# Self attention in a 6-stage decoder kernel: one PSUM bank for both halves of the transposed probabilities, three banks in rotation instead of two

## The reference, cut to what matters

```python
Q = (x @ Wq.T + bq).reshape(B, N, H, HD)
K = (x @ Wk.T + bk).reshape(B, N, H, HD)
V = (x @ Wv.T + bv).reshape(B, N, H, HD)
scores = jnp.einsum('bnhd,bmhd->bhnm', Q, K)
scores = scores * (SCALE * adaptive_scale)[None, :, None, None] / TEMP
w = jax.nn.softmax(scores, axis=-1)
attn = jnp.einsum('bhnm,bmhd->bnhd', w, V).reshape(B, N, H * HD)
y = x + (attn @ Wo.T + bo)
return (y - mu) / jnp.sqrt(var + EPS) * gamma + beta
```

## Time and profile before

| What | Value |
|---|---|
| Median of 3 runs | 1846.4 us (1839.13 to 1853.87) |
| The profiled execution, its own time | 1854.84 us |
| Its span, first to last instruction | 1853.1 us |
| Mean granted TensorE clock | 0.933 |
| Self attention, first scores to the last layer norm | about 1114 to 1605 us |
| DMA over the whole span | 8 to 9 GB/s |

### The profile page before, as it was taken

One profiled execution on the slowest core, in us unless ns is written; L12 is line 12 of the kernel. 1 busy time (PEld: TensorE's weight loads), 2 busy tenths in 40 slices (PEclk: granted clock), 3 DMA queues, 4 the chain that ended last, 5 costly groups with the idle time before them and its releaser, 6 DMA issues. The chain is left out here.

```text
span 1853.1 us, 28867 instructions
## 1 busy us (share of the span) xinstructions
PE 1646.3 (89%) x10524; PEld 949.1 (51%) x10524; DVE 1260.1 (68%) x1701; ACT 1202.8 (65%) x2569; POOL 481.8 (26%) x402
## 2 busy tenths in 40 slices
PE   5999999999999964888879798999999999789985
PEld 2343444444444422666656535666666566466654
DVE  2778777777777767888815555666666666588854
ACT  3787887787787743788772365555655556377754
POOL 2111011111111134777620002222222222155530
PEclk9999999999999975899995689999999999799977
DMA  3000001000000021000000000000000000000001
GB/s 131 1 12 1 0 7 24 0 0 0 1 0 1 0 48 30 5 6 9 2 2 1 0 1 1 1 1 1 1 1 1 1 1 1 8 8 8 2 1 46
DMA packets 30529, 16.99 MB, mean 9 GB/s; under 512 B 8545, under 2 KB 29246, under 8 KB 30398
## 3 DMA queue, kind: packets, MB, share of 16 engines
q1 hardware_dynamic: 27710, 10.52, 2.3%
q10 hardware_dynamic: 2688, 4.72, 0.7%
HBM read 13.14 MB, written 2.10 MB: 8 GB/s over the span
## 5 line engine op out<-in xcount | busy, mean ns | idle before, releaser
L2247 POOL TENSOR_TENSOR self_probs<-self_probs,self_rz 128x1024 f32<-128x1024 f32 x64 | 121.3, 1895 | 488.9 <-DVE self_rz L2278 488.9
L558 POOL TENSOR_SCALAR gru_decay<-gru_zgate 128x512 f32<-128x512 f32 x96 | 75.2, 783 | 563.1 <-ACT gru_zgate L509 537.1
L2222 ACT ACTIVATE self_probs<-self_scores,self_neg 128x128 f32<-128x128 f32 x512 | 181.4, 383 | 16.8 <-DVE self_neg L2273 16.8
L417 PE MATMUL gru_gate<-gru_xn,gru_whg 128*128 128x512 f32 x384 | 182.2, 597 | 3.5 <-DVE gru_xn L605 3.5
L421 PE MATMUL gru_hid<-gru_xn,gru_whg 128*128 128x512 f32 x384 | 180.4, 592 | 0.0
L429 PE MATMUL gru_out<-gru_y,gru_wo 128*128 128x512 f32 x384 | 178.1, 599 | 0.7 <-DVE gru_y L635 0.6
L1385 ACT ACTIVATE x_pt<-x_turned 77x512 f32<-77x512 f32 x256 | 137.6, 585 | 60.3 <-PE x_turned L1282 59.0
L1282 PE MATMUL x_turned<-const_ident,x_probs 128*77 128x128 f32 x1024 | 147.5, 290 | 20.8 <-POOL x_probs L1434 11.5
L1282 PEld LDWEIGHTS x_turned<-const_ident,x_probs 128*77 128x77 f32 x1024 | 119.6, 154 | 73.2 <-POOL x_probs L1434 25.9
L630 DVE SCALAR_TENSOR_TENSOR gru_ghid<-gru_hid,gru_half_c,gru_sighid 128x512 f32<-128x512 f32 x96 | 71.7, 747 | 107.9 <-ACT gru_sighid L510 107.8
L1491 DVE TENSOR_REDUCE x_m<-x_scores 128x16 f32<-128x1232 f32 x64 | 91.7, 1432 | 49.9 <-PE x_scores L1271 48.6
(11 more groups left out here) (440 smaller groups left out, 3507.7 us busy)
## 6 DMA issues: line engine op xcount, KB each, us to landing
gru_whg<-in_L_attn_Whg ACTq DMA_DIRECT2D x4, 768.0 KB, 9.5
x0e_ctx_in<-in_ctx SPq DMA_DIRECT2D x16, 154.0 KB
gru_xin<-in_x SPq DMA_DIRECT2D x8, 256.0 KB, 2.9
out<-moe_y SPq DMA_DIRECT2D x8, 256.0 KB, 2.2
gru_wo<-in_L_attn_Wo ACTq DMA_DIRECT2D x4, 384.0 KB, 10.6
selfe_raw<-in_L_attn_Wq SPq DMA_DIRECT2D x1, 512.0 KB, 4.5
selfe_raw<-in_L_attn_Wk SPq DMA_DIRECT2D x1, 512.0 KB, 5.7
selfe_raw<-in_L_attn_Wv SPq DMA_DIRECT2D x1, 512.0 KB, 6.8
```

Source lines behind the costliest of these rows:

```text
L417: mm(ps_gate[n % 2][:, :], whg[:, l, k, DI + c * P:DI + (c + 1) * P], xn[u][:, k, :], start=(k == 0), stop=(k == KH - 1))
L2222: last = f(probs[n % 2][:, a, jj, :], ps_s[n % 2][:, a, jj * T:(jj + 1) * T], ACT.Exp, bias=neg[n % 2][:, a, jj:jj + 1], accum_out=z[n % 2 ...
L2247: pool.tensor_tensor(probs[n % 2][:, :, :, :], probs[n % 2][:, :, :, :], whole, ALU.mult).then_inc(pn_ready.sem, 1)
```

## The change

The two banks `turned0` and `turned1` become one, `turned`; the bank set free joins the rotation, which now has three (`NBANKS`). Since both halves go through one bank, PE waits before half 1 for DVE's copy of half 0 of the same step, and before half 0 for the copy of half 1 of the step before. In `ORDER`, half 1 of `turn` moves behind `norm` x+1 and `scores` x+2. No operation is added or taken away.

```diff
-        ps_t = [t.ps(f"turned{e}", [P, 512]) for e in range(2)]
-        bank = [t.ps(f"bank{r}", [P, 512]) for r in range(2)]
+        ps_t = t.ps("turned", [P, 512])
+        NBANKS = 3
+        bank = [t.ps(f"bank{r}", [P, 512]) for r in range(NBANKS)]
...
             if now:
-                ORDER += [("turn", x, 0, 0), ("turn", x, 1, 0)]
+                ORDER += [("turn", x, 0, 0)]
             if x + 1 < LAST:
                 ORDER += [("norm", x + 1, 0, 0)]
             if later:
                 ORDER += [("scores", x + 2, 0, 0)]
+            if now:
+                ORDER += [("turn", x, 1, 0)]
...
             source = (op[0][:-4],) + op[1:]
-            r = TURN[source] % 2
-            engine.wait_ge(filled[r].sem, TURN[source] // 2 + 1)
+            r = TURN[source] % NBANKS
+            engine.wait_ge(filled[r].sem, TURN[source] // NBANKS + 1)
             return bank[r], freed[r].sem
...
                         pe.wait_ge(pn_ready.sem, n + 1)
-                        if n:
-                            pe.wait_ge(pt_ready[a].sem, n)
+
+                        if a:
+                            pe.wait_ge(pt_ready[0].sem, n + 1)
+                        elif n:
+                            pe.wait_ge(pt_ready[1].sem, n)
                         for jj in range(HALF):
-                            last = turn(ps_t[a][:, jj * T:(jj + 1) * T], probs[n % 2][:, a, jj, :], ident[:, :])
+                            last = turn(ps_t[:, jj * T:(jj + 1) * T], probs[n % 2][:, a, jj, :], ident[:, :])
```

More of the change, by code:

```diff
@@ L2010, in self_attention_stage @@
         pn_ready = t.count("pn_ready")
-        filled = [t.count(f"filled{r}") for r in range(2)]
-        freed = [t.count(f"freed{r}") for r in range(2)]
+        filled = [t.count(f"filled{r}") for r in range(NBANKS)]
+        freed = [t.count(f"freed{r}") for r in range(NBANKS)]
         sq_ready = t.count("sq_ready")
@@ L2097, in shared @@
             source = (op[0][:-4],) + op[1:]
-            r = TURN[source] % 2
-            engine.wait_ge(filled[r].sem, TURN[source] // 2 + 1)
+            r = TURN[source] % NBANKS
+            engine.wait_ge(filled[r].sem, TURN[source] // NBANKS + 1)
             return bank[r], freed[r].sem
         def taken(engine, *ops):
-            for r in range(2):
-                counts = [TURN[op] // 2 + 1 for op in ops if TURN[op] % 2 == r]
+            for r in range(NBANKS):
+                counts = [TURN[op] // NBANKS + 1 for op in ops if TURN[op] % NBANKS == r]
                 if counts:
@@ L2126, in _ @@
                     if op in TURN:
-                        r, before = TURN[op] % 2, TURN[op] // 2
+                        r, before = TURN[op] % NBANKS, TURN[op] // NBANKS
                         to = bank[r]
@@ L2280, in _ @@
                         if n >= 2 and a == 0:
-                            r, at = TURN["attend", n - 2, 0, 0] % 2, TURN["attend", n - 2, 0, 0] // 2
+                            r, at = TURN["attend", n - 2, 0, 0] % NBANKS, TURN["attend", n - 2, 0, 0] // NBANKS
                             dve.wait_ge(filled[r].sem, at + 1)
                         dve.wait_ge(turned[a].sem, n + 1)
-                        v.tensor_copy(pt[n % 2][:, a, :, :].rearrange("p j t -> p (j t)"), ps_t[a][:, :]).then_inc(pt_ready[a].sem, 1)
+                        v.tensor_copy(pt[n % 2][:, a, :, :].rearrange("p j t -> p (j t)"), ps_t[:, :]).then_inc(pt_ready[a].sem, 1)
                     elif kind == "attend_out":
```

## The result

The changed kernel took 1833.5 us (median, 1819.6 to 1841.0) beside 1849.4 us for the kernel before in the same series; the ratio is 0.9908, with a 95% interval of 0.9888 to 0.9929. That is 17 us, 0.92%, where the forecast had 19 us, 1.02%. The interval leaves out a ratio of 1, so the kernel is faster; but the gain is just short of the 1% from which the forecast would call it so. The profiled execution took 1837.25 us, against 1854.84 us.

A forecast was written before the change was run, and what follows sets the result against it. PE was taken to set the pace, losing 3.3 us per eight steps to full banks. Terms -16.5 - 6.3 + 3.0 = -19.8, taken as -19 off the 1846.4 median: 1827.4 us, range 1814 to 1848.

The forecast's parts named there:

- The middle: Six full groups of eight steps in self attention: 57.5 in place of 60.28 us each, -16.5 us in all.
- 3.3 us in eight steps are lost to full banks: PE's eight steps take 60.28 us against 57.0 unhindered; three banks were to take the full 3.3 us off.
- The new wait: Half 1 of `turn` waits for half 0's copy; the scores cover it with 0.2 us to spare, nothing charged.
- R1: Rival: no margin, PE stands 0.1 to 0.2 us before every half 1; -7 to -13, about 1836; chance 0.20.
- The one uncovered place: Step after own: DVE's late layer norm work delays half 0's copy, so half 1 waits; +0.86 us once in eight steps.
- Row maxima and ring: Maxima at A+4.0 (A: `attend`'s start), exponentials end 0.3 us later but in time; nothing charged in full groups.
- R2: Rival: exponentials, reciprocal, second copy and maxima form a ring that sets the pace; 12 us slower, 1858; chance 0.08.
- R3: Rival: weight loads stay late despite the third bank, only PE's idle part comes back; -6 us, 1840; chance 0.10.
- R4: Rival: small idle times make the granted clock fall for one step in eight; 50 us more, 1877; chance 0.02.
- Start and first group: Start of the stage and the group without own step: -1.4 up to second scores, some -4.9 after; together -6.3 us.
- its steps lose the same kind of waits: First group's steps were taken to shed bank waits by the full groups' count, shrinking by some 4.9 us.
- The end: Steps 62 and 63, without scores between halves, and the last group's late half: +1.5, +1.0, +0.8 - 0.3; together +3.0 us.

## Why the prediction came out as it did

**The middle: right, and for its reasons.** -16.3 against -16.5. By steps 24 to 31, the forecast's arithmetic gives 7.65, 6.73, 8.51, 6.73, 7.65, 7.59, 6.73 and 5.93 (so many items by 0.86, 0.96 and 1.88, and 0.86 for the stop); the trace has 7.65, 6.73, 8.57, 6.72, 7.65, 7.58, 6.72 and 5.93. The step "3.3 us in eight steps are lost to full banks" is borne out by the run with two banks: there the loads that wait for ACT are back, and 3.5 us with them. That the Trainium skill's rule on weight loads pulled ahead ("TensorE: Matmul & The Clock Gate", section "Step-by-step: what each phase is for") doesn't hold for a load with an unmet wait was rightly taken from the earlier trace rows.

**The new wait: right.** Half 1 starts at A+2.70 in the ordinary step. Its cover of 0.2 us held, so R1 (PE standing before each half 1) did not come; the run with the halves adjacent shows what was hidden, a stop of 0.94 and in all 1.18 a step. The one uncovered place was named, and came at A+3.66 for 3.6, worth 0.92 (8.57 against 7.65) for 0.86; the run with the own item's instructions later shows its cause.

**Row maxima and ring: right.** The maxima start at A+4.0 (in the step behind own, 1314.40, A+4.93), the exponentials end in time, and no ordinary step waits; R2 fell. Its mechanism is real: with the reciprocal one place further forward the kernel is slower than before.

**R3 fell** with the loads: they run 0.43 ahead. **R4 fell in the middle** of the changed kernel, whose longest stop there is 0.88. But its mechanism appears elsewhere: at the end of the changed kernel, after stops of 0.99 and 1.58 in a row, and in the variants after single stops of 1.93 and more (not after each of them). The forecast weighed the clock for the step behind own alone and not for the end.

**Start and first group: mis-sized.** The term was -6.3 with bounds -9 and -2; it measured -4.4. Its -1.4 up to the second scores was right (12.45 us before, 11.03 now), though PE, which stood for 1.47, still stands for 0.89. What failed is "its steps lose the same kind of waits", priced at -4.9: it measured -3.0. Two steps keep a wait for a full bank in spite of the third:

```profile
1120.87 1.12 PE L2144 MATMUL self_bank<-xT,selfh_w_k 128*128 128x512 f32 x2 [0.89 <-ACT selfh_qT L2214]
...
1138.86 1.09 PE L2180 MATMUL self_bank<-self_pt,self_v 128*64 128x128 f32 x16 [0.95 <-DVE self_qT L2269]
...
1167.32 1.09 PE L2180 MATMUL self_bank<-self_pt,self_v 128*64 128x128 f32 x16 [0.18 <-ACT self_v L2219]
```

In step 1 the first item, which DVE empties there, stands on DVE behind the maxima, and these behind a reciprocal that waited for the exponentials:

```profile
1136.19 0.20 DVE L2284 RECIPROCAL self_rz<-self_z 128x8 f32<-128x8 f32 x1 [1.75 <-ACT self_probs L2228]
...
1136.87 1.22 DVE L2279 TENSOR_REDUCE self_neg<-self_scores 128x8 f32<-128x1024 f32 x1
1138.00 0.80 DVE L2269 TENSOR_SCALAR self_qT<-self_bank,selfe_scale,selfe_bq 128x512 f32<-128x512 f32 x1
```

So "no bank wait is left" held for the full groups, whose emptying places it was counted from, and not for the group with one item less. By the forecast's arithmetic step 1 takes 5.86 and step 5 6.72; they take 7.13 and 7.30, which makes up the missing 1.9, and the run with the places counted anew gives 1.6 of it back.

**The end: mis-sized.** The term was +3.0 with bounds +1 and +4; it measured +4.2, just outside them. `attend` 62 came +1.50 as forecast, and the last group +0.5. What failed is step 63's "+1.0": it measured +2.8. The half did wait for the copy of the other (0.94), but the clock had fallen as well: queries and keys of the next stage and the first half of `turn` ran at 1.2 GHz. 0.7 of it came back behind `attend` 63. The forecast had priced each stop by itself and not what two in a row do to the clock.

The two misses, 1.9 and 1.2, make 3.1 of the stage's 3.3; the forecast's rounding from 19.8 to 19 and 1.2 less in the rest of the program hide a part of it in the total. The 1.2 lie within what executions differ by: in the second profile of the changed kernel the rest took 255.4, 2.0 more than before. The interval (0.7 to 1.1%) holds both the forecast's 1.02% and the 0.92%, so nothing hangs on their lying on either side of 1%; and "what a measurement of this kernel can tell from no change" was set too high, since with 16 executions of each kernel the ratio is known to 0.2%.

## What to carry to other kernels

When PE is "busy" all the time, compare distances between starts with what an instruction takes that nothing holds up: a wait that ends in time for the array can still keep a weight load from going ahead, and each such load here cost about 0.1 to 0.2 us. A bank may be taken from a double buffer if other work of PE covers the copy, here 1.1 us of scores for a copy of 0.69 behind another; then look at the places where that cover is missing, the first and the last steps and the one behind a long chain on the copying engine. Count those edges step by step, as the repeated middle is counted: both misses lay there.

## What the runs showed of the hardware that had not been expected

- Stops of PE of 0.9 to 1.3 us by themselves, even one in every step, left the granted clock at 1.00, and so did those of 1.52 and 1.47 at the start of the stage before (1.00 from 1110 to 1125 us). One of 1.97 was followed by 3.4 us at 1.2 GHz in three groups of six that are otherwise alike, at a cost of 1.6 us each; what decides between them stays open. Stops of 1.93 (halves adjacent) and of 2.05, 3.14 and 3.46 (reciprocal ahead) were followed by falls too, while one of 1.81 (reciprocal ahead, at 1558.68) was not. In each of the six profiles where two stops had only one half of `turn` between them (about 0.99 and 1.6, or 1.18 and 0.94), 3.4 or 6.8 us at 1.2 GHz began in the second or up to 1.7 us behind it.
- The stage repeats itself to 0.15 us between executions of the same kernel (469.05 and 469.20), while the program ahead of it, the same in all kernels here, moves by some 10 us (the first scores stand anywhere from 1104 to 1115 us). To judge a change of a few us in one stage the stage is to be measured in the trace; the whole time can't tell it.
